# Four norms over a graph stack: six score buffers, spread columns moved, norms of stage three shifted by a tile, four banks for the mean projections

## The reference

```python
# layer 0 (binary)
bw = sign(weight); ba = maximum(sign(x), 0)
x = layernorm(x + relu(adj @ (ba @ bw.T)))
# layer 1 (attention over the graph; h = x @ W_sa)
s_left = h @ a_sa[0, :256]; s_right = h @ a_sa[0, 256:]
e = where(adj != 0, exp(-leaky_relu(s_left[:, None] + s_right[None, :], 0.01)), 0)
x_a = (e / (sum(e, axis=1, keepdims=True) + 1e-5)) @ h
x_b = adj @ (x @ W_gcnb) + b_gcnb
attn_a = sigmoid(concat([adj @ x, x]) @ Wa.T + ba)      # attn_b: the same with Wb, bb
x = layernorm(x + sigmoid(attn_a * x_a + attn_b * x_b))
# layer 2 (mean over neighbours)
A = (adj != 0)
x = layernorm(x + A @ (x @ W + b) / sum(A, axis=0)[:, None])
# layer 3: two attention layers over all nodes, softmax(scores) * adj
x = layernorm(x + gat(gat(x, W_stack[0], adj), W_stack[1], adj))
```

## Time and profile before

| | |
|---|---|
| median of 3 runs | 531.64 us (530.36 to 535.01) |
| the profiled execution's own time | 533.75 us |
| its span in the profile | 532.0 us |
| PE busy | 495.4 us, 93% |
| DVE / ACT / POOL busy | 352.7 / 244.5 / 172.2 us |
| mean granted TensorE clock | 0.965 of full |

### The profile page before, as it was taken

One profiled execution on the slowest core, in us unless ns is written; L12 is line 12 of the kernel. 1 busy time (PEld: TensorE's weight loads), 2 busy tenths in 40 slices (PEclk: granted clock), 3 DMA queues, 4 the chain that ended last, 5 costly groups with the idle time before them and its releaser, 6 DMA issues.

```text
span 532.0 us, 5688 instructions
## 1 busy us (share of the span) xinstructions
PE 495.4 (93%) x1901; PEld 312.0 (59%) x1901; DVE 352.7 (66%) x751; ACT 244.5 (46%) x446; POOL 172.2 (32%) x175
## 2 busy tenths in 40 slices
PE   5799999999999799998999999999999999999890
PEld 4799854446654477777655445555556545554580
DVE  5789879917999537838432953962742595566866
ACT  5467459954884333342334533433324564342200
POOL 3211334502434305653100631441330262434511
PEclk9799999999999679999999999999999999999896
DMA  8556200001451000000000000000000000000101
GB/s 304 184 179 210 75 31 0 0 0 57 156 207 30 1 0 1 0 1 1 1 0 0 1 0 1 2 0 0 0 1 0 1 1 2 0 0 0 41 17 49
DMA packets 8148, 20.68 MB, mean 39 GB/s; under 512 B 976, under 2 KB 4708, under 8 KB 8120
## 3 DMA queue, kind: packets, MB, share of 16 engines
q1 hardware_dynamic: 6840, 18.75, 10.6%
q0 software_dynamic: 464, 0.79, 0.5%
q10 hardware_dynamic: 816, 0.79, 0.5%
HBM read 18.94 MB, written 1.39 MB: 38 GB/s over the span
## 4 chain that ended last, share of the span: by engine, by line
PE 70%; DVE 17%; issue 3%; POOL 3%; ACT 3%; DMA 3%; POOLq 0%; DVEq 0%; ACTq 0%
PE psum L1416 17%; PE psum L1463 15%; PE psum L1202 9%; PE psum L1178 5%; DVE eb L815 4%; PE psum L1396 3%; PE psum L1238 3%; PE psum L1534 3%; PE psum L1123 2%; DMA Wsa<-in_L_gnn_W_sa_dram 2%; PE psum L1370 2%; PE psum L1498 2%; DVE stats L757 1%; DVE eb L812 1%; PE psum L1349 1%
## 5 line engine op out<-in xcount | busy, mean ns | idle before, releaser
L1416 PE MATMUL psum<-QT,xT 128*128 128x512 f32 (+3 forms) x264 | 107.7, 543 | 0.3 <-DVE xT L997 0.3
L1463 PE MATMUL psum<-ST,Wh 128*128 128x512 f32 (+3 forms) x220 | 94.9, 563 | 1.6 <-DVE vbuf L979 1.1
L405 POOL TENSOR_TENSOR es<-es,ST 128x512 f32<-128x512 f32 (+3 forms) x60 | 72.3, 1205 | 59.1 <-ACT ST L594 57.4
L1416 PEld LDWEIGHTS psum<-QT,xT 128*128 128x128 f32 (+1 forms) x264 | 48.2, 186 | 47.2 <-issue 40.7
L581 ACT ACTIVATE ST<-psum 128x512 f32<-128x512 f32 (+3 forms) x66 | 36.1, 547 | 86.2 <-DVE rm L930 80.9
L930 DVE TENSOR_TENSOR rm<-psum,rm 128x512 f32<-128x512 f32 (+3 forms) x60 | 37.4, 623 | 46.7 <-PE psum L1416 46.7
L1463 PEld LDWEIGHTS psum<-ST,Wh 128*128 128x128 f32 (+1 forms) x220 | 40.8, 190 | 40.4 <-issue 33.2
L357 POOL TENSOR_TENSOR rstd<-veps,nhalf 128x1 f32<-128x1 f32 (+1 forms) x44 | 28.1, 638 | 100.4 <-DVE veps L760 100.3
L1238 PE MATMUL psum<-eb,x_all 128*128 128x512 f32 (+3 forms) x132 | 56.8, 579 | 0.9 <-ACT eb L469 0.9
L373 POOL TENSOR_TENSOR esumb<-esumb,eb 128x1354 f32<-128x1354 f32 (+1 forms) x10 | 35.6, 3559 | 58.6 <-ACT eb L469 58.6
L952 DVE TENSOR_TENSOR ST<-ST,psum 128x512 f32<-128x512 f32 (+3 forms) x66 | 39.9, 614 | 17.6 <-PE psum L1445 17.6
(11 more groups left out here) (164 smaller groups left out, 775.2 us busy)
## 6 DMA issues: line engine op xcount, KB each, us to landing
adj_rows<-in_adj_dram SPq DMA_DIRECT2D x10, 677.0 KB, 4.3
rows<-in_adj_dram SPq DMA_DIRECT2D x10, 677.0 KB, 4.1
out_dram<-xs SPq DMA_DIRECT2D x10, 128.0 KB, 1.7
x_all<-in_x_dram SPq DMA_DIRECT2D x2, 512.0 KB, 6.5
W<-in_L_gnn_W_stack_dram SPq DMA_DIRECT2D x2, 512.0 KB, 5.5
adj_rows<-in_adj_dram SPq DMA_DIRECT2D x1, 338.5 KB
rows<-in_adj_dram SPq DMA_DIRECT2D x1, 338.5 KB
w0n<-in_L_gnn_weight_dram ACTq DMA_DIRECT2D x1, 256.0 KB, 4.9
```

What stands on the lines that cost most here:

```text
L405: nc.gpsimd.tensor_tensor(es[0:r, g % 2, 0:w], es[0:r, g % 2, 0:w], buf(g)[0:r, j, 0:w], ALU.add)\
L1416: last = nc.tensor.matmul(psum[0:r, SB[n % 3], 0:w], xT[l][:, k, j * P:j * P + r], QT[:, k, c0:c1], start=(k == 0), stop=(k == KD - 1))
L1463: last = nc.tensor.matmul(bank(AB[g] + m, 0, w), Wh[g // NC][0:r, j, m * P:(m + 1) * P], buf(g)[0:r, j, 0:w], start=(j == 0), stop=(j == T ...
```

## The change

- **Ring of six.** `RING` is 6. The two new score buffers lie where mask buffers lay; the masks are laid out anew, three masks are made after the scores, the fourth after the degrees. Six scores are made before the 22 dot products, five after them. ACT does two column degrees ahead of each of the first six exponentials. `z_proj` comes twice after `h_part` 1 and 2 and once after each later one.
- **Spread columns and weights.** DVE's products with `Wsa` and `Ub` (`dot_columns`) stand ahead of `finish_a(1)`; PE's spread (`spread_dots`) stands inside `agg_a(2)`, ahead of its step 8, and writes bank 3; ACT copies it to `ubc` after `adj_evac(3)`; the left dot products begin at tile 3, two there. `Wsa` is issued on ACT's queue after the `posT` copies, `Wg` after `adj_evac(1)`, with a semaphore each; nine small loads of POOL's wait until tile 1 of adj is transposed. The six `xw` copies are split between DVE and ACT; `positive(2)` stands ahead of `lower_bits(0)`.
- **Norms of stage three.** DVE takes `attn_out(i+1)` ahead of `norm_apply(i)`, and `attn_sum` three tiles ahead; POOL takes `rsqrt(i+1)` ahead of `low_half(i)`; `LEAD` is 4.
- **Four banks.** `c_proj` goes through banks 6, 7, 0, 1 and waits for the statistics of the tile four before.

```diff
-    RING = 4
+    RING = 6
+    CB = [6, 7, 0, 1, 6, 7, 0, 1, 6, 7, 6]
...
+            pool.wait_ge(adjT_turned.sem, 2 * BANKS_T)
             for n, w in enumerate((wa, wb)):
...
+            rsqrt(NB, 0)
             for i in range(T):
-                rsqrt(NB, i)
+                if i + 1 < T:
+                    rsqrt(NB, i + 1)
                 low_half(i)
...
             for j in range(RING):
-                col_degree(2 * j)
+                for n in range(2 * j, min(2 * j + 2, T)):
+                    col_degree(n)
                 exp_scores(j)
-                col_degree(2 * j + 1)
...
             for i in range(T):
+                if i == 1:
+                    dot_columns()
                 finish_a(i)
-                if i == 0:
-                    dve.wait_ge(ubc_ps.sem, 1)
-                    nc.vector.tensor_copy(ubc[:, :, :], bank(7).rearrange("p (h n) -> p h n", h=2)).then_inc(ubc_ready.sem, 1)
+                if i == 3:
                     dve.wait_ge(ubc_ready.sem, 1)
-                else:
-                    left_dot(i - 1)
+                    left_dot(0)
+                if i >= 3:
+                    left_dot(i - 2)
...
+            def dot_columns():
+
+                dve.wait_ge(a_in.sem, 16)
+                dve.wait_ge(wsa_in.sem, 16)
...
             attn_sum(0)
             attn_sum(1)
+            attn_out(0)
+            attn_sum(2)
             for i in range(T):
-                attn_out(i)
-                if i + 2 < T:
-                    attn_sum(i + 2)
+                if i + 1 < T:
+                    attn_out(i + 1)
                 norm_apply(NB, i, vbuf[0:kk(i), i % 4, :])
+                if i + 3 < T:
+                    attn_sum(i + 3)
                 if i + 4 < T:
                     mean_mask(i + 4)
...
+            def spread_dots():
+
+                pe.wait_ge(ub_ready.sem, 2 * KD)
+                pe.wait_ge(adjT_banks_read.sem, 3 * BANKS_T + 1)
+                for half in range(2):
+                    for k in range(KD):
+                        last = nc.tensor.matmul(bank(3, half * D + k * P, half * D + (k + 1) * P), Ub[:, half, k, :],
+                                                ident[:, :], start=True, stop=True)
+                last.then_inc(ubc_ps.sem, 1)
...
                 for k in range(T):
+                    if i == 2 and k == CROSS:
+                        spread_dots()
...
-                for _ in range(2):
+                for _ in range(2 if j <= 2 else 1):
                     if i < T and j >= 1:
                         z_proj(i)
                         i += 1
...
-            LEAD = 3
+            LEAD = 4
...
-                if i >= 2:
-                    pe.wait_ge(NM.var_ready.sem, i - 1)
+                if i >= 4:
+                    pe.wait_ge(NM.var_ready.sem, i - 1 if i == T - 1 else i - 3)
```

More of the change, by code:

```diff
@@ L732, in _ @@
             positive(1)
+            positive(2)
             lower_bits(0)
-            positive(2)
-            for t0 in range(0, T, 2):
+            for t0 in range(0, T, 4):
                 t1 = min(t0 + 2, T)
@@ L740, in _ @@
             lower_bits(1)
-            dve.wait_ge(a_in.sem, 16)
-            dve.wait_ge(w_in.sem, 16 * 2)
-            for half in range(2):
-                for k in range(KD):
-                    own.link(nc.vector.tensor_tensor_reduce(out=dots[:, 0, :], in0=Wsa[:, k, :],
-                                                            in1=a_b[:, half * D:(half + 1) * D], scale=-1.0, scalar=0.0,
-                                                            op0=ALU.mult, op1=ALU.add, accum_out=ucol[:, half, k:k + 1]))
-            for half in range(2):
-                for k in range(KD):
-                    nc.vector.tensor_scalar(Ub[:, half, k, :], Ub[:, half, k, :], ucol[:, half, k:k + 1], None, ALU.add)\
-                        .then_inc(ub_ready.sem, 1)
             def norm_stats(nm, i, v):
@@ L782, in dot @@
                                                op0=ALU.mult, op1=ALU.add, accum_out=dst[0:r, :]).then_inc(dots_done.sem, 1)
+            def dot_columns():
[3 more added lines that the diff above has]
+                    for k in range(KD):
+                        own.link(nc.vector.tensor_tensor_reduce(out=dots[:, 0, :], in0=Wsa[:, k, :],
+                                                                in1=a_b[:, half * D:(half + 1) * D], scale=-1.0, scalar=0.0,
+                                                                op0=ALU.mult, op1=ALU.add, accum_out=ucol[:, half, k:k + 1]))
+                for half in range(2):
+                    for k in range(KD):
+                        nc.vector.tensor_scalar(Ub[:, half, k, :], Ub[:, half, k, :], ucol[:, half, k:k + 1], None, ALU.add)\
+                            .then_inc(ub_ready.sem, 1)
             def left_dot(i):
@@ L851, in _ @@
                 i += 1
-            for j in range(4):
+            for j in range(3):
                 mean_mask(j)
@@ L867, in _ @@
                 .then_inc(rdeg_ready.sem, 1)
+            mean_mask(3)
             dve.wait_ge(den_ps.sem, 1)
@@ L1183, in _ @@
                 agg_a(i)
-                if i == 0:
-                    pe.wait_ge(ub_ready.sem, 2 * KD)
-                    for half in range(2):
-                        for k in range(KD):
-                            last = nc.tensor.matmul(bank(7, half * D + k * P, half * D + (k + 1) * P), Ub[:, half, k, :],
-                                                    ident[:, :], start=True, stop=True)
-                    last.then_inc(ubc_ps.sem, 1)
                 if i + 2 < T:
@@ L1334, in _ @@
             mul_w3(1)
+            h_proj(3)
             for j in range(T):
```

61 lines of the change are left out of this document (42 added, 19 removed).

## The result

The changed kernel takes 514.32 us (median of four runs, 513.07 to 516.05) beside 532.1 us of the kernel before in the same measurement: ratio 0.966, 95% interval 0.961 to 0.972. Six more executions on another occasion gave 516.21 (514.42 to 518.33), ratio 0.970, 0.967 to 0.973; of all ten the median is 515.5. The forecast was 512, with the range 505 to 519. The profiled execution of the first measurement, with a span of 511.3 us, is the shortest of the ten, 513.07 us; what is read from it is read from the best case.

The account below looks back on a forecast made before the run. PE, busy for 93% of the span, bounds the kernel with its matmuls, waits and clock. Terms 4.3 + 10.9 + 1.8 + 1.7 + 1.3 = 20.0 us, off 533.75 and 531.64, give 513.8 and 511.6; forecast 512, range 505 to 519.

Parts of the forecast that it names:

- stage one: From the start to the first `h_part`: spread columns' wait and slow clock go, less small new waits; 4.3 us, bounds 1.5 to 5.8.
- stage two: First `h_part` to first `h_proj`: two late waits and the half clock behind them go; 10.9 us, bounds 4.6 to 11.5.
- turnover: First `h_proj` to first `c_part`: full clock, less newly visible DVE work and one more `h_proj`; 1.8 us, bounds -0.7 to 3.5.
- aggregation: First `c_part` to first `c_proj`: DVE no longer stands for POOL's root; 33.9 for 35.55 us, 1.7 gained, bounds 0 to 2.7.
- mean projections: First `c_proj` to `q_mul`: four waits of 1.5 us go, small waits at `turn_mean(1)` come; 1.3 us, bounds 0.5 to 1.5.
- Rival A: Clock falls in the turnover all the same, some 9 us of matmuls at half speed; costs 5 us, 517; chance 0.15.
- B: DVE takes PE's place: stage one gives only 1.5 us, the aggregation nothing; 4.5 us less gain, 516; chance 0.12.
- C: The reverse: DVE keeps up in stage one and the aggregation; 508 us; chance 0.10.
- D: In stage two DVE loses 5 us more, last exponential late, clock falls, half of 10.9 + 1.8 comes; 518 to 523; chance 0.05.
- E: Slower than before: stage one's new waits at every tile bring the clock down and keep it there; 547 us; chance 0.03.

Follow-up runs that it names:

- fillers: The kernel before with five additional unused matmuls (128x512) where PE waits for POOL's last sum, nothing else changed: 526.79 us, ratio 0.989.

## Why the prediction came out as it did

By its own steps, each from the profiled pair:

| step | predicted | measured |
|---|---|---|
| stage one | 4.3 | 116.19 - 111.88 = 4.3 |
| stage two | 10.9 | 72.91 - 62.24 = 10.7 |
| turnover | 1.8 | 13.06 - 11.49 = 1.6 |
| aggregation | 1.7 | 35.55 - 32.58 = 3.0 |
| mean projections | 1.3 | 18.64 - 17.49 = 1.15 |
| sum | 20.0 | 20.7 |

**Right for its reasons.** The two large terms, the places, and nearly all that would be late next hold. That the sum meets the profiled pair within 0.7 us is in part luck: the profile before has both falls of the clock at the greatest length seen in any trace, and the one after has none. In stage one the remaining waits are 0.5 for `Ub` and 0.8 for `lo`, 1.3 us for the 1.5 counted. POOL's loads delay the first norm by 1.3 us, for the 1 us counted. In stage two DVE stands at its second `zp_evac` for 2 and 4 us after scores 8 and 9, as counted; these are the rows of the changed kernel:

```profile
140.04 0.42 DVE L846 TENSOR_TENSOR xb<-psum,b1b 128x256 f32<-128x256 f32 x1 [1.96 <-PE psum L1294]
...
150.87 0.42 DVE L846 TENSOR_TENSOR xb<-psum,b1b 128x256 f32<-128x256 f32 x1 [4.29 <-PE psum L1294]
...
176.06 0.48 DVE L909 SCALAR_TENSOR_TENSOR vbuf<-psum,coef,xb 128x256 f32<-128x256 f32 x1 [0.22 <-DVE coef L902]
```

The last of them is the first use of the coefficients: 176.06, or 180.4 on the old axis (4.3 us later), for a predicted 180.7.

**The term that was mis-sized** is the aggregation, 3.0 us for 1.7 and outside its bounds of 0 to 2.7. I had PE's floor of 32.9 us from the earlier trace rows, and added a microsecond because DVE's work is "close to 3.3 us a tile against PE's 3.33". A period of DVE just under PE's costs nothing once PE has a tile in hand; that is what the lead is for, and the aggregation took 32.58 us, a little less even than that floor. I also took the order and the lead as two separate small helps, where the runs show that neither works alone.

**What the sum didn't hold** is that a profiled execution's clock is a draw. Taken from the medians, the change gives 16 to 18 us and not 20.7, and the forecast of 512 is 2 to 4 us too low. Rival A named it, the clock falls in the turnover all the same, at 0.15 and with a price of 5 us, as a choice between two cases. The first profile shows the sign of the forecast, a full clock from 172 to 190 us; the second, of the same kernel, shows that of A, a low clock behind 172 us without a wait for `esumb`. The fall comes in one of the two profiles of the changed kernel and in seven of the eight of its variants without the old wait. From `h_part` to `c_part`, 3.4 us of it cost 1.4 us (75.15 for 73.73), and 6.8 us cost 2.2 with the old norms (75.91) and 2.9 with the old stage one (76.58). It was less a rival than a term of its own. In the same way 2.8 of stage one's 4.3 us were the clock after one wait in one execution.

**The other rivals.** B, DVE in PE's place: not in stage three, where PE is busy for 32.00 of 32 us, and not in stage one, where the waits for `lo` are 0.8 us. Its mechanism is there, on both engines. These rows of the second profile are DVE's mask, POOL's `low_half` and DVE's `attn_out`:

```profile
185.74 0.86 DVE L857 TENSOR_SCALAR maskT<-adjT 128x1354 fp32r<-128x1354 f32 x1
185.76 1.42 POOL L382 TENSOR_TENSOR xhl<-x_all,xhl 128x256 fp32r<-128x256 f32 x1 [1.09 <-ACT xhl L549]
186.51 0.95 DVE L918 SCALAR_TENSOR_TENSOR vbuf<-vbuf,xp 128x256 f32<-128x256 f32 x1
```

`low_half` takes 1.42 us beside the mask, and 0.73 where DVE is idle; `attn_out`, behind the mask and beside `low_half`, takes 0.95 us, and 0.41 elsewhere. The same section of the Trainium skill (SBUF — State Buffer, Who interferes with whom) has a rule for each: the one of the prediction for `attn_out`, with its two inputs, and for the mask, which reads one tensor, that a `tensor_scalar` can enter a mode in which DVE takes both ports and blocks GpSimd for the whole instruction. The trace agrees with both: the mask passes its 1354 elements in 0.86 us, where an instruction with two inputs takes 1.63 for as many. It costs nothing here as long as PE has a tile in hand. C, DVE keeps up in stages one and three: it does in stage three, for 1.3 us more than forecast, and not in stage one. D, stage two doesn't get ahead: refuted, no wait for `esumb` remains. E, a clock that falls and stays low through short waits in stage one: refuted, the clock is 1.00 from 20 to 62 us, with the waits for `Ub` and `lo` in it.

## What to carry to other kernels

Read a wait of TensorE together with the granted clock behind it: a gap cost its own length once and, where the clock fell, more behind it: some 3 us behind the 3.10 in the profile before, and some 8, half of 17, behind the 3.69. But behind the wait of stage one the second part came in two executions of three, so it belongs in a forecast as a share, and a single profile must be compared by its landmarks and clock with a second one of the same kernel before a microsecond or two is read from it. Where an order is shifted by a tile on one engine, ask which other engine's lead it draws on; the two are tested together or not at all.

## What was not expected of the hardware

- The same wait of 3.1 us of PE, in three executions of stage one in its old form, was followed by 6.8, 3.4 and 0 us of half clock.
- The clock also fell without a wait in front, at the end of stage two, where PE is recorded as busy throughout: for 3.4 or 6.8 us, in eight of the ten profiles of the changed kernel and its variants that have no wait for POOL's sum. Whether the one-column matmuls bring it is open.
- A f32 matmul of 512 columns, five of which stand as ten records in the row of fillers, takes 0.86 us from one start to the next, and one on reduced formats in `c_part` 0.24 at most: eight of 512 and four of 330 columns take 2.57 us, from `c_part` at 203.37 to the next `h_proj` at 205.94.
- Where DVE and POOL meet in SBUF, both pay: `low_half` 1.42 us for 0.73, `attn_out` 0.95 for 0.41.
